# First expert loop: the expert's weights as the stationary operand of the up products

## The reference, cut to what matters

```
tw = routing_weights(xf)                      # 4 (expert, weight) pairs per row, 16 experts
for e in range(16):
    h = silu(xf @ W1[e]) * (xf @ W3[e])       # 128 -> 512
    out = out + tw[:, e:e + 1] * (h @ W2[e])  # 512 -> 128
```

## Time and profile before

| | us |
|---|---|
| time, median of 3 runs | 1066.12 (1065.29 to 1070.09) |
| span of the profiled execution | 1011.2 |
| median less span, which lies outside the profiled instructions | 54.9 |
| first to last matmul of the first expert loop | 241.2 to 455.1 |
| start of its last scatter | 456.1 |
| PE busy over the span | 857.5 (85%) |
| DVE busy | 753.3 (74%) |
| ACT busy | 520.8 (52%) |
| POOL busy | 361.6 (36%) |

### The profile page before, as it was taken

How to read it: one execution, slowest core, us unless ns; L and a number is a source line. 1 busy time by engine, 2 the same in 40 slices (tenths; PEclk the granted TensorE clock), 3 DMA queues, 4 the chain that set the end, 5 groups by cost and what they waited for, 6 DMA issues and landing times.

```text
span 1011.2 us, 44652 instructions
## 1 busy us (share of the span) xinstructions
PE 857.5 (85%) x17239; PEld 684.5 (68%) x17239; DVE 753.3 (74%) x3032; ACT 520.8 (52%) x1605; POOL 361.6 (36%) x565
## 2 busy tenths in 40 slices
PE   4666777736899999985799999999999999999595
PEld 2245554513566666662699999999999999976253
DVE  4348897698777676677788888888888888887244
ACT  0535766603666666653355555555555555555073
POOL 0306675565667777750111111111111111100644
PEclk9767998656999999996899999999999999998597
DMA  7710002320122222315200000000000000002133
GB/s 229 277 51 1 1 1 94 129 67 27 42 75 77 77 77 77 77 41 174 86 4 0 0 0 0 0 0 0 0 0 0 0 0 0 0 2 64 42 96 114
DMA packets 30137, 50.64 MB, mean 50 GB/s; under 512 B 7969, under 2 KB 19161, under 8 KB 30074
## 3 DMA queue, kind: packets, MB, share of 16 engines
q1 hardware_dynamic: 23578, 36.95, 11.2%
q0 software_dynamic: 6496, 12.84, 4.7%
HBM read 38.40 MB, written 11.38 MB: 49 GB/s over the span
## 4 chain that ended last, share of the span: by engine, by line
PE 41%; POOL 3%; DVE 3%; issue 2%; DMA 1%; ACT 1%; DVEq 0%; POOLq 0%; SPq 0%
PE quad L1456 20%; PE bank L1456 17%; POOL y_scratch L1759 2%; POOL x_scratch L1753 1%; PE quad L1471 1%; PE bank L1471 1%; DVE post L1616 0%; PE quad L1782 0%; ACT post L1567 0%; PE bank L1444 0%; DVE post L1655 0%; DVE post L1630 0%; DVE post L1624 0%; DVE post L1644 0%; DMA post<-y_scratch 0%
## 5 line engine op out<-in xcount | busy, mean ns | idle before, releaser
L1456 PE MATMUL quad<-post,area 128*128 128x32 f16 (+1 forms) x7520 | 237.4, 182 | 3.2 <-DVE post L1661 2.1
L1456 PEld LDWEIGHTS quad<-post,area 128*128 128x128 f16 x7520 | 217.3, 96 | 17.4 <-DVE post L1661 9.0
L1456 PE MATMUL bank<-post,area 128*128 128x32 f16 (+1 forms) x6260 | 193.4, 180 | 4.7 <-DVE post L1661 2.8
L1456 PEld LDWEIGHTS bank<-post,area 128*128 128x128 f16 x6260 | 176.0, 96 | 17.8 <-DVE post L1661 3.4
L1409 POOL COPY post<-post 128x32 f32 (+1 forms) x126 | 28.6, 227 | 341.6 <-DVE post L1661 341.6
L1553 ACT ACTIVATE post<-post 128x96 f32<-128x96 f32 x252 | 71.4, 283 | 130.9 <-DVE post L1616 130.9
L1616 DVE TENSOR_REDUCE post<-quad 128x96 f32<-128x192 f32 x378 | 99.7, 264 | 3.0 <-PE quad L1456 2.6
L1616 DVE TENSOR_REDUCE post<-bank 128x96 f32<-128x192 f32 x378 | 99.3, 263 | 3.1 <-PE bank L1456 1.5
L885 POOL DMA_INDIRECT y_scratch<-area x78 | 76.9, 986 | 43.0 <-DVE area L1272 23.8
L1567 ACT ACTIVATE post<-post 128x32 f32<-128x32 f32 x252 | 57.8, 229 | 64.5 <-DVE post L1630 64.5
L880 POOL DMA_INDIRECT area<-x_scratch,area x78 | 78.3, 1003 | 28.3 <-issue 21.3
(11 more groups left out here) (328 smaller groups left out, 1756.5 us busy)
## 6 DMA issues: line engine op xcount, KB each, us to landing
w0s<-in_w SPq DMA_DIRECT2D x12, 768.0 KB
area<-in_rec SPq DMA_DIRECT2D x7, 640.0 KB
post<-y_scratch SPq DMA_DIRECT2D x8, 504.0 KB
area<-in_w SPq DMA_DIRECT2D x4, 768.0 KB
area<-in_f SPq DMA_DIRECT2D x2, 1024.0 KB, 7.4
area<-in_patches SPq DMA_DIRECT2D x1, 1488.4 KB
x_scratch<-post SPq DMA_DIRECT2D x1, 1472.0 KB, 7.2
area<-in_taps SPq DMA_DIRECT2D x1, 1350.0 KB
```

Of the source, the lines that this page charges most:

```text
L1456: mm = pe.matmul(at[0][:, at[1] + out.start:at[1] + out.stop], rec_w[:, w, s, m * P:(m + 1) * P], operand, start=False, stop=False, skip_g ...
```

## The change

`up` swaps its operands: 128x128 pieces of the expert's weights become the stationary operand, and the turned rows (128 columns) move. The four pieces of the hidden width lie side by side in the same PSUM bank, so the gated rows come out already turned, `turn_hidden` goes, and `high` and `low` read `hid` in SBUF in place of a PSUM bank. The two PSUM banks of the turned hidden values become a second bank for the turned rows and a second one for the result of `down`, and the waits for these two are one tile looser.

```diff
-        T_bank = bank[4].bitcast(F16)[:, 0:XW2]
-        hidT_bank = [bank[5 + u][:, 0:H0] for u in range(2)]
-        y_bank = bank[7][:, 0:2 * D].rearrange("p (s d) -> p s d", s=2)
+        T_banks = [bank[4 + u].bitcast(F16)[:, 0:XW2] for u in range(2)]
+        y_banks = [bank[6 + u][:, 0:2 * D].rearrange("p (s d) -> p s d", s=2) for u in range(2)]
...
             def turn(i):
                 pe.wait_ge(sg(f"xg{i % XG}"), 16 * (i // XG + 1))
-                if i >= 1:
-                    pe.wait_ge(sg("xT"), i)
+                if i >= 2:
+                    pe.wait_ge(sg("xT"), i - 1)
...
-            def up(i, out, wh, wl, name):
+            def up(i, out, r, first, name):
 
                 xh, xl = xT[:, i % 4, 0:D], xT[:, i % 4, D:2 * D]
-                pe.matmul(out, xh, wh, start=True, stop=False, skip_group_check=True)
-                pe.matmul(out, xl, wh, start=False, stop=False, skip_group_check=True)
-                pe.matmul(out, xh, wl, start=False, stop=True, skip_group_check=True).then_inc(sg(name), 1)
-
-            def turn_hidden(i):
-
-                pe.wait_ge(sg("gated"), i + 1)
-                if i >= 2:
-                    pe.wait_ge(sg("hid_low"), i - 1)
                 for c in range(C0):
-                    mm = pe.transpose(hidT_bank[i % 2][:, c * P:(c + 1) * P], hid[:, i % 2, c * P:(c + 1) * P], ident)
-                mm.then_inc(sg("turned_ps0"), 1)
+                    acc = out[:, c * P:(c + 1) * P]
+                    wh, wl = (w0s[:, bass.ds(r + s * W0 + first + c * P, P)] for s in range(2))
+                    pe.matmul(acc, wh, xh, start=True, stop=False, skip_group_check=True)
+                    pe.matmul(acc, wh, xl, start=False, stop=False, skip_group_check=True)
+                    mm = pe.matmul(acc, wl, xh, start=False, stop=True, skip_group_check=True)
+                mm.then_inc(sg(name), 1)
 
             def down(i, weights):
                 pe.wait_ge(sg("hid_low"), i + 1)
-                if i >= 1:
-                    pe.wait_ge(sg("y_sb"), i)
+                if i >= 2:
+                    pe.wait_ge(sg("y_sb"), i - 1)
+                y_bank = y_banks[i % 2]
...
-                if 1 <= i <= NT:
-                    turn_hidden(i - 1)
...
             def high(i):
-                act.wait_ge(sg("turned_ps0"), BATCH + i + 1)
+                act.wait_ge(sg("gated"), i + 1)
                 if i >= 2:
                     act.wait_ge(sg("y_ps"), i - 1)
-                act.activation(hidT[:, i % 2, 0, :], hidT_bank[i % 2], ACT.Copy).then_inc(sg("hid_high"), 1)
+                act.activation(hidT[:, i % 2, 0, :], hid[:, i % 2, :], ACT.Copy).then_inc(sg("hid_high"), 1)
...
             def low(i):
                 dve.wait_ge(sg("hid_high"), i + 1)
-                dve.tensor_tensor(hidT[:, i % 2, 1, :], hidT_bank[i % 2], hidT[:, i % 2, 0, :], ALU.subtract
+                dve.tensor_tensor(hidT[:, i % 2, 1, :], hid[:, i % 2, :], hidT[:, i % 2, 0, :], ALU.subtract
                                   ).then_inc(sg("hid_low"), 1)
...
                     if i >= 2:
-                        dve.wait_ge(sg("turned_ps0"), BATCH + i - 1)
+                        dve.wait_ge(sg("hid_low"), i - 1)
```

More of the change, by code:

```diff
@@ L939, in turn @@
                 pe.wait_ge(sg(f"xg{i % XG}"), 16 * (i // XG + 1))
-                if i >= 1:
-                    pe.wait_ge(sg("xT"), i)
+                if i >= 2:
+                    pe.wait_ge(sg("xT"), i - 1)
                 for s in range(2):
-                    mm = pe.transpose(T_bank[:, s * D:(s + 1) * D], xg[:, i % XG, s * D:(s + 1) * D], ident16)
+                    mm = pe.transpose(T_banks[i % 2][:, s * D:(s + 1) * D], xg[:, i % XG, s * D:(s + 1) * D], ident16)
                 mm.then_inc(sg("xT_ps"), 1)
@@ L994, in ffn_pe @@
                         pe.wait_ge(sg("silu"), i - 1)
-                    up(i, bank[i % 2], *(w0s[:, bass.ds(r + s * W0, H0)] for s in range(2)), "gate_ps")
+                    up(i, bank[i % 2], r, 0, "gate_ps")
                     if i >= 2:
                         pe.wait_ge(sg("gated"), i - 1)
-                    up(i, bank[2 + i % 2], *(w0s[:, bass.ds(r + s * W0 + H0, H0)] for s in range(2)), "up_ps")
+                    up(i, bank[2 + i % 2], r, H0, "up_ps")
                     if i + 1 < NT:
                         at_of[i + 1] = expert_of(i + 1)
-                if 1 <= i <= NT:
-                    turn_hidden(i - 1)
                 if i >= DOWN_LAG:
@@ L1061, in turned @@
                     act.wait_ge(sg("up_ps"), i - 3)
-                act.activation(xT[:, i % 4, :], T_bank, ACT.Copy).then_inc(sg("xT"), 1)
+                act.activation(xT[:, i % 4, :], T_banks[i % 2], ACT.Copy).then_inc(sg("xT"), 1)
             def high(i):
-                act.wait_ge(sg("turned_ps0"), BATCH + i + 1)
+                act.wait_ge(sg("gated"), i + 1)
                 if i >= 2:
                     act.wait_ge(sg("y_ps"), i - 1)
-                act.activation(hidT[:, i % 2, 0, :], hidT_bank[i % 2], ACT.Copy).then_inc(sg("hid_high"), 1)
+                act.activation(hidT[:, i % 2, 0, :], hid[:, i % 2, :], ACT.Copy).then_inc(sg("hid_high"), 1)
             for i in range(PE_AHEAD):
@@ L1271, in keep @@
                     dve.wait_ge(sg(f"y_out{i % YR}"), 16 * (i // YR))
-                dve.tensor_reduce(y_sb[:, i % YR, :], y_bank.rearrange("p s d -> p d s"), AX, ALU.add
+                dve.tensor_reduce(y_sb[:, i % YR, :], y_banks[i % 2].rearrange("p s d -> p d s"), AX, ALU.add
                                   ).then_inc(sg("y_sb"), 1)
```

## The result

| | before | after | ratio (95% interval) |
|---|---|---|---|
| first timing, us | 1065.84 (1065.29 to 1070.09) | 1106.84 (1100.33 to 1111.01) | 1.0356 (1.0312 to 1.040) |
| timed again, chip B | 1014.45 (13 runs) | 1062.06 (4 runs) | 1.0468 (1.0449 to 1.0487) |
| timed again, chip C | 1065.37 (7 runs) | 1107.19 (4 runs) | 1.0394 (1.0356 to 1.0433) |

The change makes the kernel slower by 41 to 48 us. Two of the chips used (call them A and B) ran the kernel before in 1014 to 1016 us and two (C and D) in 1061 to 1065, the same program each time. By its span of 1011 the profile of before is of the first kind; the times beside it and the first profile after are of the second.

The account below looks back on a forecast made before the run. PE's instruction queue was to become the bound at 3.19 us a tile: first loop +37.6 us and end -1.5 make +36, so 1102 us against 1066.1, range 1085 to 1125.

Parts of the forecast that it names:

- The queue becomes the bound: First expert loop: PE's instruction queue, 20 register operations at 0.124 us, needs 3.19 us a tile, above POOL's 2.57; chance 0.72.
- The tile's size: First expert loop: a tile goes from 2.50 to 3.19 us, 75 tiles and the last up product taking 241.4 us.
- Matmuls of 128 columns at 0.056: Up products: 24 matmuls with their own weight loads at 0.056 us cost PE 1.34 us in place of 1.30.
- high, low, second banks, late experts: First expert loop: hid read from SBUF, looser waits and late experts' extra weights change nothing at a 3.19 us tile.
- Start: Start of the first expert loop, on a slow clock: the first two tiles keep their time, to 246.65 us.
- End: End of the first loop, last up product to last scatter: about 1.5 us less, without turning back.
- The base: Whole kernel: 54.9 us of the median 1066.1 lie outside the 1011.2 us span and do not change.
- Rival, clock: Rival with chance 0.10: a slow clock in the first expert loop; its sign is a granted clock below 1.00 after 260 us.
- signs of being wrong: Up-product matmuls 0.056 apart throughout, POOL with issue gaps alone, period 2.6 to 2.8 us; or clock below 1.00 after 260 us.
- Rivals, POOL: First expert loop: register operations hide and POOL's two DMAs set a 2.57 us period, 13 us less, 1053; chance 0.07.
- POOL with `low`: First expert loop: `low` with two SBUF inputs holds POOL's DMA some 0.2 us, period 2.77, 1066, no change; chance 0.05.
- Rival, partly hidden: First expert loop: part of the register operations hides, period 2.6 to 3.0 us, 1075 to 1090 us; chance 0.06.

Follow-up runs that it names:

- e2: Kernel before, operand roles and turning back kept, each up product cut into four 128-column pieces with a register address each: 1078.62 us, ratio 1.0626.
- e3: Kernel before with the up products cut into the same four pieces, but always reading expert 0's weights at fixed addresses: 1018.91 us, ratio 1.0045.
- e4: Changed kernel with the low halves of the up products' weights read at a fixed address, 12 register operations a tile: 1014.59 us, ratio 1.0007.
- e6: Changed kernel with the down products reading expert 0's weights at a fixed address, 16 register operations a tile: 1028.5 us.
- a0: Changed kernel, run again unaltered on chip B: 1062.06 us, ratio 1.0468.
- e1: Changed kernel with both up products always reading expert 0's weights at fixed addresses: 1014.66 us, ratio 0.999.
- c0: Kernel before, unchanged, run again on chip A with a profile: 1015.89 us, ratio 0.9998.
- c1: Kernel before, unchanged, run with a profile on chip D: 1060.51 us.
- a1: Changed kernel, run once more unaltered on chip C: 1107.19 us, ratio 1.0394.
- e5: Changed kernel with up products at fixed addresses, gated rows in two PSUM banks, one bank each for turned rows and result: 1005.71 us, ratio 0.991.

## Why the prediction was right, and where it was not

- **The queue becomes the bound.** Right. The step of 0.124 is right to the third digit, and the steps of a tile sum to 3.17 against 3.19 to 3.20 predicted. e2, e3, e4 and e6 show it from four sides; e2 with e3 and a0 with e4 are the clean pairs, each on one chip.
- **The tile's size.** Some steps are longer than the bare one: the register operations of the up products come 0.131 apart on average, and 27 steps of the whole loop take 0.25 to 0.28. That makes 3.33 in place of 3.19, and over 75 tiles +10.7 us. It is the mis-sized term, and it is why the forecast of +36 is a quarter short. With it and the end below the sum becomes +47; chip B measures +47.6. Why single steps are longer stays open.
- **Matmuls of 128 columns at 0.056.** Right, 0.06 within each piece above. Where nothing holds PE up in e1 a tile takes 2.13 (some 30 of its 77), predicted as PE's own 2.11.
- **high, low, second banks, late experts.** Worth nothing under the queue, as said: `low` 681 ns, and at 20 operations a tile POOL's transfers are not longer either (988 ns in a0).
- **Start.** Nearly right: the last up matmul of the second tile starts 5.2 after the loop's first in a0, and 4.9 after it in before and c0. The clock is granted at half there, until 246.6 in before and 247.6 in a0. In that time the pieces of three matmuls in a0 start 0.32 apart, 2.56 for the eight of a tile, where six matmuls of 512 columns at 0.42 make 2.5. Two register operations are 0.25, so PE and not its queue is the bound there.
- **End.** From the last load of an expert's number to the last scatter 9.3 before and 8.2 on chip B: -1.1 where -1.5 was predicted.
- **The base.** Wrong. I put 54.9 us outside the span, to fit a profile of 1011 to a median of 1066. Time less span is 1.9 in c0. The 50 us were another kind of chip, with the first loop at 3.24 a tile instead of 2.70 (c1). That 1102 lies close to the measured 1106.8 is partly luck: on that kind of chip before loses about 50 and after about 45, so the difference of 41 lies near the predicted 36, while the tile is 3.81 there and not 3.19.
- **Rival, clock, given 0.10.** On chip B the clock is full from 250 us on, so a slower clock in the loop plays no part there. On the second kind of chip it is granted at half for 34 us of the loop (first profile) and 31 (a1), in spells of 3.4 or 6.8; in the 3.4 us ahead of each of the first profile's nine PE stood idle for 1.3 us or more in all (1.34 to 2.38). Yet in c1, where PE once stood idle for 2.70 of 3.4 us, there is no such spell, so idle time alone isn't shown to bring one. A granted clock below 1.00 after 260 us was one of the prediction's signs of being wrong, and there it came. How much of the 3.81 is the spells' was not separated.
- **Rivals, POOL, and POOL with `low`.** Not what bounds the change. But e1 and e5 show both as the next bound: with the queue freed the exchanged roles give 1014.7, no change, and 1005.7 once `low` has one SBUF input. The hold that `low` puts on POOL has its number here: a median of 1.24 for e1's transfers that begin in `low`, in place of 0.97 in c0, and none over 0.99 in e5 once one input is in PSUM.
- **Rival, partly hidden.** Its times don't follow from its periods: by the prediction's own sum 2.6 a tile gives 1058 and 3.0 gives 1088, where it says 1075 to 1090. Nothing hangs on it, as the period is 3.33.

## What to carry to other kernels

Count what an operand's register address costs in the engine's queue, 0.124 us per address here, and compare that sum with the engine's own work: cutting the up products into four pieces with an address each took their 4 register operations a tile to 16, 0.50 to 1.98 us, and the busy time didn't show it. The sign in these profiles is a PE whose busy share falls (10.00 to 8.74 of 10 us) though nothing it waits for is late, and whose matmul count per stretch is lower than the same matmuls reach without the registers (1020 in a0 beside 1253 in e4 over 300 to 400 us). Before adding a profile's span to a timing, check that the two belong together: 55 us that no row explains are a warning, not a constant.

## What the runs showed that I had not expected

- The same program took 1014 to 1016 us on two chips and 1061 to 1065 on two others, most of it in the loop where POOL's indirect transfers run back to back (38.8 of 42 for the kernel before, 36 of 45 for the changed one). In c1 28 of 78 of PE's increments are answered 2.2 us late or more, nearly all of these 0.9 after the end of a POOL instruction. The stage of L1449 in the kernel after, whose loop has no indirect transfer, takes 421 and 422 us on the two kinds (first to last weight load for `quad` 577.1 to 998.4, and 540.3 to 962.5).
- In e1 the POOL transfers that begin inside `low`, with its two SBUF inputs, are longer (a median of 1.24 us beside 0.97 in c0), and 38 of the 45 end 0.84 to 0.87 after the operation does, wherever in it they began: 399.75 is the end of `low` and 400.59 of the fetch in e1. That is nearly a whole transfer of 0.97, as if it had only started then.
